# A test-time-training attention scan: projections reordered, first model made by the vector engine, inverse root moved to the Pool engine, last stores moved

## The reference

```python
XQ, XK, XV = proj_heads(q_w), proj_heads(k_w), proj_heads(v_w)
eta = token_idx * sigmoid(X @ ttt_lr_weight + ttt_lr_bias) / HD
def _ln_fused_l2_bwd(x, target, gamma, beta):
    mu = x.mean(-1); std = sqrt(x.var(-1) + EPS); xh = (x - mu) / std
    gxh = (gamma * xh + beta - target) * gamma
    return (D * gxh - gxh.sum(-1) - xh * (gxh * xh).sum(-1)) / (D * std)
def step(carry, x):                       # one minibatch of 16 tokens
    W1_s, b1_s = carry; xq, xk, xv, eta_mb = x
    Z1 = xk @ W1_s + b1_s
    grad = _ln_fused_l2_bwd(Z1, xv - xk, ln_w, ln_b)
    Attn1 = tril(xq @ xk.T)
    b1_bar = b1_s - tril(eta_mb) @ grad
    Z1_bar = xq @ W1_s - eta_mb * Attn1 @ grad + b1_bar
    W1_new = W1_s - (last_eta * xk).T @ grad
    b1_new = b1_s - sum(last_eta * grad)
    return (W1_new, b1_new), xq + _ln(Z1_bar, ln_w, ln_b)
out = _ln(all ys, post_norm_weight, post_norm_bias) @ o_w.T
```

## Time and profile before

| what | us |
|---|---|
| median of 3 runs (lowest to highest) | 1247.74 (1244.07 to 1251.53) |
| the profiled execution's own time | 1246.01 |
| its span in the trace | 1244.2 |
| TTT: first block | 0 to 55.3 |
| TTT: scan | 55.3 to 212.4 |
| TTT: outputs | 212.4 to about 363 |
| everything after | about 363 to 1244.2 |

### The profile page before, as it was taken

The page is one execution under the profiler, slowest core; times in us unless marked ns, Lnnn a source line. Parts: engine busy times, 40 slices in busy tenths (PEclk is TensorE's granted clock), DMA queues, the critical chain, the costliest instruction groups (busy, mean ns, idle before and its releaser), DMA issues. The chain is left out here.

```text
span 1244.2 us, 24092 instructions
## 1 busy us (share of the span) xinstructions
PE 1069.2 (86%) x8893; PEld 658.7 (53%) x8908; DVE 850.6 (68%) x1996; ACT 582.1 (47%) x1582; POOL 272.0 (22%) x342
## 2 busy tenths in 40 slices
PE   8478883999978999889898978779999998779965
PEld 4255662777743333335556447567777775334422
DVE  2279874799966888658997598734467878733325
ACT  2134532454426666655453427257777774322212
POOL 6200110011110111313433110300000001146842
PEclk9789875999989999999999999989999999889977
DMA  5713344000011242070000000167000000659466
GB/s 172 118 41 95 97 111 127 2 3 2 2 52 52 77 125 84 27 130 19 1 1 1 2 2 18 69 202 221 18 18 18 23 26 22 186 149 268 84 123 260
DMA packets 82703, 94.80 MB, mean 76 GB/s; under 512 B 19664, under 2 KB 66263, under 8 KB 82327
## 3 DMA queue, kind: packets, MB, share of 16 engines
q1 hardware_dynamic: 73548, 79.79, 22.1%
q0 software_dynamic: 6368, 9.50, 4.1%
q10 hardware_dynamic: 2672, 3.98, 0.9%
HBM read 68.65 MB, written 21.97 MB: 73 GB/s over the span
## 5 line engine op out<-in xcount | busy, mean ns | idle before, releaser
L401 DVE TENSOR_REDUCE gqa_x_slots<-gqa_scores 128x8 f32<-128x1024 f32 x64 | 78.4, 1226 | 30.7 <-PE gqa_scores L288 21.8
L1571 DVE TENSOR_REDUCE mla_neg_max<-mla_scores 128x8 f32<-128x1024 f32 x32 | 39.2, 1225 | 77.2 <-PE mla_scores L1436 51.7
L1518 ACT ACTIVATE mla_probs<-mla_scores,mla_neg_max 128x128 f32<-128x128 f32 x256 | 90.1, 388 | 0.0
L358 ACT ACTIVATE gqa_expT<-gqa_scoresT 128x1024 f32<-128x1024 f32 x64 | 65.5, 1024 | 48.4 <-PE gqa_scoresT L309 48.4
L309 PE MATMUL gqa_scoresT<-gqa_x_slotsT,gqa_keys 32*128 32x512 f32 x256 | 73.9, 649 | 9.1 <-issue 4.0
L288 PE MATMUL gqa_scores<-gqa_keys_bd,xT 32*128 32x512 f32 x256 | 74.5, 686 | 2.7 <-DVE gqa_x_slots L401 1.4
L1426 PE MATMUL mla_q_ps<-xT,mla_merged_home 128*128 128x128 f32 x512 | 64.4, 280 | 1.6 <-PEq L63 1.6
L1426 PEld LDWEIGHTS mla_q_ps<-xT,mla_merged_home 128*128 128x128 f32 x512 | 61.3, 196 | 2.2 <-issue 1.9
L1459 PE MATMUL mla_out_ps<-mla_merged_home,mla_attT 128*128 128x256 f32 x256 | 60.7, 380 | 0.7 <-ACT mla_attT L1531 0.7
L1518 ACT ACTIVATION_READ_ACCUMULATOR mla_probs<-mla_scores,mla_neg_max 128x1 f32 x256 | 58.4, 228 | 0.0
L2600 PEld LDWEIGHTS ttt_z_ps<-ttt_g_pairs,ttt_masked 128*64 128x64 f32 x1024 | 51.5, 137 | 11.5 <-issue 10.4
(11 more groups left out here) (468 smaller groups left out, 2639.9 us busy)
## 6 DMA issues: line engine op xcount, KB each, us to landing
moe_w_gu<-in_moe_w_gu SPq DMA_DIRECT2D x24, 384.0 KB
gqa_keys_bd<-in_gqa_keys_bd SPq DMA_DIRECT2D x16, 512.0 KB, 3.4
moe_w_dn<-in_moe_w_down SPq DMA_DIRECT2D x24, 192.0 KB
moe_sums<-moe_zeros SPq DMA_DIRECT2D x2, 2176.0 KB, 11.5
ttt_by_token<-ttt_tokens_lanes SPq DMA_DIRECT2D x4, 576.0 KB, 4.5
ttt_lanes<-ttt_by_token SPq DMA_DIRECT2D x16, 144.0 KB, 5.4
xT<-in_x_feat SPq DMA_DIRECT2D x4, 512.0 KB
x_tok<-in_mla_woT SPq DMA_DIRECT2D x8, 256.0 KB, 3.2
```

Of the source, the lines that this page charges most:

```text
L358: nc.scalar.activation(expT[:, k % 2, 2 * u:2 * u + 2, :], scoresT[:], ACT.Exp, scale=HD ** -0.5).then_inc(exp_ready, 1)
L401: nc.vector.tensor_reduce(x_slots[:, b % 2, :, c * NJ + 2 * half:c * NJ + 2 * half + 2, HD].rearrange("p g j -> p j g"), scores[:, of].rea ...
L1518: ins = nc.scalar.activation(probs[:, k % NB, e, i, :], scores[:, k % 2, e, i, :], ACT.Exp, bias=neg_max[:, k % 2, e, i:i + 1], accum_out= ...
```

## The change

It leaves the arithmetic as it is, but for the way the inverse root is computed. In order of the program:

1. First block: the order of PE's jobs becomes keys of groups 0 and 1, all 16 lane jobs, keys of groups 2 and 3. The first keys wait for half of the weight load. `by_token` has no memory of its own, it lies in `g_pairs`. SP stores groups 0, 1, 2, loads the lanes of X = 0, stores group 3; the loads of X = 1 stand at the head of the scan block, and nothing waits for the loads at the block's end. DVE waits for them where it reads them.
2. ACT lays the keys of n = 0 in the first block. DVE fills `g_sum` with the bias and makes the first masked model from `w0_own`, twice 128x1024. PE's `start` comes after the first two `outputs` and `turn_keys`.
3. The sum of gradients in `g_sum` now holds the bias and is scaled: POOL multiplies each gradient by minus the last token weight (`g_last`) and adds it. `outputs` begins with one matmul on it, instead of one on the bias and one at the end on the sum.
4. The inverse root: POOL adds epsilon and takes the power -0.5 (`invert`, two instructions of 128x32), where ACT and DVE took a root, a reciprocal and a Newton step. The variance of the other half is summed by DVE two instructions before the end of a step. POOL also clears `g_pairs` (128x8192) between the first and the second `invert`.
5. The end of the scan: `x` is loaded ahead of the bias stores; the last store of gradients is split by half, that of X = 1 is issued in the third block, and PE waits there for each half (new line 2635). `keep_busy` has two matmuls, not four.

```diff
+by_token = g_pairs[:].rearrange("p h b q e -> p (h b q e)")[:, 0:B * QQ * LANE].rearrange("p (b q e) -> p b q e", b=B, q=QQ)
...
-JOBS = [(job, g, i) for g in range(NG) for job, n in (("k", DH), ("lane", NG)) for i in range(n)]
...
+JOBS = [(job, g, i) for job, gs, n in (("k", (0, 1), DH), ("lane", (0, 1, 2, 3), NG), ("k", (2, 3), DH)) for g in gs for i in range(n)]
...
     store(0)
     store(1)
-    load(0)
     store(2)
+    load_lanes(sp, 0)
     store(3)
-    load(1)
-    sp.wait_ge(lane_loaded, 16 * 2 * NG * QQ)
 
...
+    nc.gpsimd.memset(k_bd[:], 0.0).then_inc(keys_zeroed, 1)
+    nc.gpsimd.memset(w_middle[:], 0.0)
...
-    nc.gpsimd.memset(k_bd[:], 0.0)
-    nc.gpsimd.memset(g_pairs[:], 0.0)
-    nc.gpsimd.memset(w_middle[:], 0.0)
-    nc.gpsimd.memset(g_sum[:], 0.0)
...
+    for g in range(2):
+        keep_keys(g)
+    for g in range(2):
         sigmoids(g)
+    act.wait_ge(keys_zeroed, 1)
+    act.wait_ge(proj_copied, 2 * DH)
+    lay_keys(0, 0)
+    for g in range(2, NG):
+        sigmoids(g)
+    for g in range(2, NG):
+        keep_keys(g)
+    act.wait_ge(proj_copied, NG * DH)
+    lay_keys(1, 0)
     act.wait_ge(set_, 1)
     nc.scalar.activation(unused[:], eps[:], ACT.Sqrt)
...
+    nc.vector.tensor_copy(g_sum[:].rearrange("p x b e -> p (x b) e"), b0_lanes[:].unsqueeze(1).to_broadcast([P, NG, LN]))
+    first = [P, NG * 2, DH, P // QQ]
+    for X in range(2):
+        tt(model[:, X].rearrange("p (r c f) -> p r c f", c=DH, f=P // QQ), w0_own[:].unsqueeze(1).to_broadcast(first), own_head[:].unsqueeze(1).unsqueeze(1).to_broadcast(first), ALU.mult)
...
+    load_lanes(sp, 1)
     latent.sync(sp, *merged, 0, 1)
     store_bias(0)
-    for n in range(NC):
+    sp.wait_ge(pairs_zeroed, 1)
+    for n in range(NC - 1):
         if n and 2 * n < latent.SLOTS:
             latent.sync(sp, *merged, 2 * n, 2 * n + 1)
         if n:
-            store_gradients(n - 1)
-        if n == NC - 1:
-            store_bias(1)
+            for X in range(2):
+                sp.wait_ge(grads_ready[X], n)
+            store_gradients(sp, n - 1, slice(0, 2), g_stored[(n - 1) % SLOTS_G])
         if 2 * n + 1 < latent.SLOTS:
             latent.sync(sp, *merged, 2 * n + 1, 2 * n + 2)
     sp.dma_start(keep["x_tok"][:], io["x"].rearrange("b t d -> t b d")).then_inc(x_loaded, 16)
+    store_bias(1)
+    for X in range(2):
+        sp.wait_ge(grads_ready[X], NC - 1)
+    store_gradients(sp, NC - 2, slice(0, 2), g_stored[(NC - 2) % SLOTS_G])
     sp.wait_ge(w_stored, 16 * NH * PARTS * QQ)
     sp.dma_start(biases[:], b_dram.rearrange("h q b l e -> (h q) (b l e)")).then_inc(w_fetched, 16)
-    store_gradients(NC - 1)
+    sp.wait_ge(grads_ready[0], NC)
+    store_gradients(sp, NC - 1, slice(0, 1), last_stored[0])
     for slot in range(SLOTS_G):
-        sp.wait_ge(g_stored[slot], 16 * NG * QQ * len(range(slot, NC, SLOTS_G)))
+        sp.wait_ge(g_stored[slot], 16 * NG * QQ * len(range(slot, NC - 1, SLOTS_G)))
     sp.wait_ge(w_fetched, 16)
-    sp.wait_ge(x_loaded, 16)
...
+    def invert(X, n):
+        pool.wait_ge(var_ready[X], n + 1)
+        nc.gpsimd.tensor_scalar(var_eps[:, X], var[:, X], 1.0 / HD, EPS, ALU.mult, ALU.add).then_inc(eps_added[X], 1)
+        pool.wait_ge(eps_added[X], n + 1)
+        nc.gpsimd.tensor_tensor(rstd[:, X], var_eps[:, X], keep["neg_half"][:].to_broadcast([P, NR]), ALU.pow).then_inc(rstd_ready[X], 1)
+
...
+        need(pool, sum_kept[1 - X], n + X)
+        nc.gpsimd.tensor_scalar(g_last[:], g_now[:, n % SLOTS_G, X], neg_last[:], None, ALU.mult).then_inc(scaled[X], 1)
+        pool.wait_ge(scaled[X], n + 1)
+        need(pool, sum_kept[X], n)
...
-        nc.gpsimd.tensor_tensor(total, total, g_now[:, n % SLOTS_G, X], ALU.add).then_inc(sum_kept[X], 1)
+        nc.gpsimd.tensor_tensor(total, total, g_last[:], ALU.add).then_inc(sum_kept[X], 1)
...
+    invert(0, 0)
+    for g in range(NG):
+        pool.wait_ge(lane_stored[g], 16)
+    nc.gpsimd.memset(g_pairs[:], 0.0).then_inc(pairs_zeroed, 1)
...
+    for n in range(NC):
         for X in range(2):
+            if 2 * n + X + 1 < 2 * NC:
+                invert(1 - X, n + X)
+            if n == NC - 1:
+                continue
             keep_sum(X, n)
...
     def outputs(X, n):
         need(pe, z_copied[1 - X], n + X)
-        nc.tensor.matmul(z_ps1[:, X].rearrange("p (g e) -> p g e", g=2), same_lane[:], b0_lanes[:].unsqueeze(1).to_broadcast([P, 2, LN]), start=True, stop=False, skip_group_check=True)
-        pe.wait_ge(masked_ready[X], n + 1)
+        need(pe, sum_kept[X], n)
+        nc.tensor.matmul(z_ps1[:, X], same_lane[:], g_sum[:, X].rearrange("p b e -> p (b e)"), start=True, stop=False, skip_group_check=True)
+        if n == 0:
+            pe.wait_ge(keys_laid[X], 1)
+        need(pe, masked_ready[X], n)
         for g in range(2):
             for c in range(DH):
                 for b4 in range(NG):
                     at = (g * DH + c) * (P // QQ)
-                    nc.tensor.matmul(z_ps1[b4 * 32:(b4 + 1) * 32, X, at:at + P // QQ], k_bd[:, X, n % 2, c, g, b4].rearrange("p q t -> p (q t)"),
-                                     model[:, X, b4 * 256 + at:b4 * 256 + at + P // QQ], start=False, stop=False, skip_group_check=True)
-        need(pe, sum_kept[X], n)
-        nc.tensor.matmul(z_ps1[:, X], neg_lane[:], g_sum[:, X].rearrange("p b e -> p (b e)"), start=False, stop=True, skip_group_check=True).then_inc(z_ready[X], 1)
+                    ins = nc.tensor.matmul(z_ps1[b4 * 32:(b4 + 1) * 32, X, at:at + P // QQ], k_bd[:, X, n % 2, c, g, b4].rearrange("p q t -> p (q t)"),
+                                     model[:, X, b4 * 256 + at:b4 * 256 + at + P // QQ], start=False, stop=(g == 1 and c == DH - 1), skip_group_check=True)
+        ins.then_inc(z_ready[X], 1)
 
     def update(X, n):
...
+    def variance(X, n):
+        dve.wait_ge(squared[X], n + 1)
+        tr(var[:, X], rows(sq[:, X]), AX_X, ALU.add).then_inc(var_ready[X], 1)
+
+    def gradients(X, n):
         z, u, x_hat, gx, gxx = zu[:, X, 0], zu[:, X, 1], xg[:, X, 0], xg[:, X, 1], xg[:, X, 2]
         now, g = slice(2 * X, 2 * X + 2), g_now[:, n % SLOTS_G, X]
-        dve.wait_ge(squared[X], n + 1)
-        tr(var[:, X], rows(sq[:, X]), AX_X, ALU.add).then_inc(var_ready[X], 1)
+        s = 2 * n + X
         dve.wait_ge(z_copied[X], n + 1)
         order(tt(by_seq(u), by_seq(z), gamma2[:].unsqueeze(1).to_broadcast([P, 2, LN]), ALU.mult))
-        dve.wait_ge(std_ready[X], n + 1)
-        order(refined_rstd(nc, order, rstd[:, X], std[:, X], var_eps[:, X], spare[:, X]))
+        dve.wait_ge(rstd_ready[X], n + 1)
         order(tt(xg[:, X, 0:2].rearrange("p a (r o) -> p a r o", o=HD), zu[:, X].rearrange("p a (r o) -> p a r o", o=HD),
                  rstd[:, X].unsqueeze(1).unsqueeze(3).to_broadcast([P, 2, NR, HD]), ALU.mult))
+        dve.wait_ge(lane_loaded[X], 16 * NG * QQ)
         order(tt(by_seq(gx), by_seq(gx), lanes[:, n, now, 0:LN], ALU.add))
-        if between:
-            between()
+        if s and s < 2 * NC - 1:
+            mask_model(1 - X, n + X)
         order(tt(gxx, gx, x_hat, ALU.mult))
         order(tr(sums[:, X, 1], rows(gxx), AX_X, ALU.add))
         stt(by_seq(coef[:, X]), lanes[:, n, now, LN:], 1.0 / HD, by_seq(rstd[:, X]), ALU.mult, ALU.mult)
         order(tt(rows(gxx), rows(x_hat), wide(sums[:, X, 1]), ALU.mult))
         order(stt(gx, gxx, -1.0 / HD, gx, ALU.mult, ALU.add))
         order(tr(sums[:, X, 0], rows(gx), AX_X, ALU.add))
+        if s < 2 * NC - 1:
+            variance(1 - X, n + X)
         order(stt(rows(gx), wide(sums[:, X, 0]), -1.0 / HD, rows(gx), ALU.mult, ALU.add))
         need(dve, g_stored[n % SLOTS_G], 16 * NG * QQ * (n // SLOTS_G))
         tt(rows(g), rows(gx), wide(coef[:, X]), ALU.mult).then_inc(grads_ready[X], 1)
 
-    mask_model(0, 0)
-    mask_model(1, 0)
+    variance(0, 0)
     for n in range(NC):
-        gradients(0, n, (lambda: mask_model(1, n)) if n else None)
...
+store_gradients(sp, NC - 1, slice(1, 2), last_stored[1])
...
+    if b % (B // 2) == 0 and u == 0:
+        pe.wait_ge(last_stored[b // (B // 2)], 16 * NG * QQ)
...
-keep_busy(nc, z_ps[:, 1, :], keep["ident"][:], k_feat[:, 0, 0:512], 4)
+keep_busy(nc, z_ps[:, 1, :], keep["ident"][:], k_feat[:, 0, 0:512], 2)
...
+    if b == 0:
+        dve.wait_ge(x_loaded, 16)
```

143 lines of the change are left out of this document (68 added, 75 removed).

## The result

The changed kernel takes 1269.0 us (median of 4 runs, 1266.3 to 1275.7) where the one before takes 1247.8: the ratio is 1.0178, with a 95% interval of 1.0124 to 1.0232. It is slower, by 1.8%. The forecast was 1228, faster, and the time lies inside the range of 1212 to 1272.

The account below looks back on a forecast made before the run. First block bound by a chain of transfers, regular scan steps by DVE's own instructions, the end by transfers. Second gradient -20.7, steps +9.4, end -6.5 and -2 sum to -19.8 us on 1246.0: forecast 1228, range 1212 to 1272.

Parts of the forecast that it names:

- p: Length of POOL's power on 32 columns, within each root: taken as 1.85 us, with ends of 0.69 and 4.9.
- Scan's start: End of the first block: the scan begins near 40.0 us instead of 55.3, no longer waiting for lane loads.
- Second gradient: Start of the scan: second gradient starts at 57.2 + 2p, so at 60.9 us instead of 81.6, -20.7.
- Regular step: Scan: the chain through POOL's root sets each step at 6.93 + p, 8.8 us instead of 7.77.
- the hindrance: Regular scan step: POOL's scaling and sum run against DVE's two-input instructions and lengthen its chain by 1.05 us.
- Long steps: Scan: of 10.7 us extra in a few long steps, about 5 disappear inside the slower steps, 9 at p = 4.9.
- End: After the last gradient: SP's reordered stores let the third block begin 4 us after it, a net gain of 6.5.
- rival 1: Scan: every power column costs like the second, p = 4.9, steps of 11.8 us, kernel 1268, slower; chance 0.29.
- Two matmuls fewer: Head of the third block: two useless matmuls less are 2.9 us, taken as a gain of 2.
- Rival 3: Scan's second step: late loads of X = 1 make DVE wait 5 us, kernel 1233; chance 0.07.
- The rule weighed: Scan: POOL instructions hold the port shared with DVE for their whole length; step 0.45 us longer, sum 6 more.
- the middle of two ends: Forecast case for the whole kernel: p = 1.85, the geometric middle of 0.69 and 4.9, giving 1228 us; chance 0.42.

Follow-up runs that it names:

- experiment 3: The kernel before the change, with an unused power of 1 to 32 columns behind each of POOL's 14 sums: 1247.4 us, ratio 1.0007.
- experiment 6: The changed kernel with the power on 8 of the 32 columns, the other roots staying 1: 1223.4 us, ratio 0.9778.
- experiment 1: The changed kernel with the old root (ACT's deviation, DVE's reciprocal and Newton step), early variance kept: 1214.3 us, ratio 0.9765.
- experiment 9: The changed kernel with old root, SP's last transfers reordered, gradients summed unscaled and two matmuls at the head of `outputs`: 1215.2 us, ratio 0.976.
- experiment 8: The changed kernel with the old root and without POOL's scaling of the gradients, which are summed unscaled: 1217.9 us, ratio 0.9733.
- 7: The changed kernel with the old root, second bias parts stored two steps earlier, x loaded behind the first half of the last gradients: 1218.7 us, ratio 0.9737.
- experiment 11: The changed kernel with the old root, the same kernel as in experiment 1, run again on another chip: 1216.1 us, ratio 0.9764.

## Why the prediction was wrong

**The term that failed is p.** I had bounds of 0.69 and 4.9 from the rows of one and two columns, and took "the geometric middle of the ends, 1.85", with the argument that "the cost per column fell from one to the next". That argument gave nothing: a fixed part and a constant cost per column make two such rows as well. The only slope that the trace had, 0.141, gave 4.9, and I set it aside for a middle that no row supports. Measured are 0.158 a column and 5.6 in all, 14% above even my upper end: a difference of two short instructions (547 and 688 ns) is a poor measure of a slope, and by experiment 3 the same width varies by up to 0.19. POOL's sum over 256 columns in 0.73 us, my other argument, has another operation, and says nothing of the power.

**The rest of the sum, with p = 5.6 put in.** The start and the end held, the steps came out shorter than my formula.

- Scan's start: 40.0 expected, PE's first matmul at 40.38.
- Second gradient: 57.2 + 2p is 68.1 with the measured 5.46 and 5.43; it came at 67.97.
- Regular step: 6.93 + p is 12.53; measured 12.08. Of the 0.45, 0.28 are the hindrance, 0.22 + 0.55 = 0.77 where I put 1.05, and most of the rest lies between the variance and DVE's first use of the root: 1.02 besides the power where I put 1.17. The shape, DVE idle until POOL's root, is as I had it. Experiment 6 confirms it at another p: a step of 8.31 where my formula gives 8.75.
- Long steps: I let 9 of the 10.7 us vanish at p = 4.9. From the second gradient to the last but one, 13 steps take 157.85 against 13 x 12.08 = 157.04, so only 0.8 of it is left. The last step has no mask and takes 9.87, which my sum counted as a full one.
- End: third block 0.4 after the last gradient, as rival 1 had it ("SP is always done before DVE", 10.6 gained). With a short power SP is the later one: 7.2 in experiment 6, where the forecast had 4. Two matmuls fewer: 5.85 against 3.68, 2.2 for my 2.
- Rival 3 (lanes of X = 1 late) did not occur: they were issued at 41.76, and in the scan DVE waits long only for the root. In experiment 1 DVE reads them already at 52.30, and does not wait for them there either.

**Rival 1's number is in part luck.** Its sum was +20.5, with p = 4.9. Measured are -13.6, +48.2 and -12.6, +22.0 at the first scores, and the medians differ by 21.2. But with p = 5.6 my own formula gives -13.5, then 14 x (12.53 - 7.77) less the 9, +57.6, and -12.6, so +31.5, or 1279. A power 0.7 too short hid steps that the formula had too long, 9.4 in 14 of them (5.0 in the first 13, 2.7 in the last, 1.7 in the long steps).

**The clock.** That the single profile shows 29.7 is for the most part the stretch with the fall of the clock in the third block (+8.3), for which I had no term.

**The rule weighed** was rightly left out of the sum: DVE's multiply beside the power took 0.46, 0.04 more than its like, and in experiment 3 the eleven instructions that began behind the widest power's start and before 130 kept their lengths.

**Where the chance went wrong.** Rival 1 had the only measured slope for it and got 0.29, the middle of two ends 0.42. When the sign of the sum turns at p = 3.4 and the only two rows point to 4.9, the slower case should have been the likeliest.

**Still open:** what brings TensorE's clock down for some 10 us in the third block. The fall 16 us behind the first scores was in both profiles of the changed kernel and in that of experiment 9, and in none of the single profiles with four useless matmuls (10), with whole stores (4) or with the clearing moved (2); the old root had none there in two profiles. One profile each is too little to name a cause, and no median separates these. Whether the scaling (experiment 8) and the tail (7) are worth their 0.3% each is open too, and so is the difference of up to 8 us between profiles in the part of the kernel that the change leaves alone.

## What to carry to other kernels

Before an operation is put into a chain that goes round once a step, time it at its full width, or take the slope that the trace has, however poor, rather than a middle between bounds. An operation that hinders nobody and relieves the busiest engine can still lose: what counts is its latency against what it replaces, here 5.6 us for 1.06 of DVE and 0.6 of ACT beside it (two instructions of 0.32 and 0.31 in the step of the earlier trace rows). When a change has several parts, look at them apart: this one held a gain of 2.4% and a loss of 4.2%, and the version with the old root (0.9765 and 0.9764 of before) beats both kernels. A time that a rival's sum hits is no proof of that sum: put the measured term in and see whether it still does.

## What the runs showed of the hardware

- POOL's power costs 0.4 to 0.55 us and 0.158 us for each column of 128 partitions, nearly in a straight line from 2 to 32 columns (experiment 3); its sum of two tiles costs under 3 ns a column (0.72 us for 256). That is more than fifty times between two operations of one instruction form.
- A power of 5.6 us on POOL leaves DVE's instructions at their lengths, two-input ones too, but for 0.04 in the one that it begins under, while a POOL sum or scaling lengthens them (0.42 to 0.97 us, 0.69 to 0.91). The scaling of 128x256 took 0.93 to 1.03 us beside DVE, where I had put 0.40 from a copy; what it takes with DVE idle no row shows.
- TensorE's granted clock fell to 0.5 for about 10 us in the midst of a stretch in which PE was busy 9.5 to 10 us of 10, in both profiles of the changed kernel and in experiment 9. Another fall, at 324 to 330 in experiment 11, is absent from the profile of the same kernel in experiment 1.
